# A mixture-of-experts layer whose sorted rows carry the data of both results, routed in parts of 5 and 3 sequences, with the next scan's first inputs and the last sums behind the last block

## What is computed

```python
scores = sigmoid(xf @ gate_w + bias)
top_scores, top_idx = top_k(scores, 2)
top_scores = top_scores / (sum(top_scores) + 1e-06)
w = zeros((T, 8)).at[arange(T)[:, None], top_idx].add(top_scores)
hact = gelu(einsum('th,ehi->tei', xf, up_w) + up_b)          # 8 experts, 128 -> 512
eo = einsum('tei,eih->teh', hact, down_w) + down_b           # 512 -> 128
combined = einsum('teh,te->th', eo * 0.1, w)
shared = (gelu(xf @ sw_up + sb_up) @ sw_down + sb_down) * 0.1
out = shared + combined
out = out / (max(abs(out), axis=-1) + 1e-06)                 # then x = x + 0.5 * out
```

## Time and profile before

| | us |
|---|---|
| median of 3 runs | 1491.89 (1487.93 to 1494.34) |
| the profiled execution's own time | 1493.21 |
| its span (first to last instruction) | 1490.9 |
| PE busy | 1261.4 (85%) |
| DVE busy | 967.9 (65%) |
| ACT busy | 830.7 (56%) |
| POOL busy | 685.2 (46%) |

### The profile page before, as it was taken

The page is one execution under the profiler, slowest core; times in us unless marked ns, Lnnn a source line. Parts: engine busy times, 40 slices in busy tenths (PEclk is TensorE's granted clock), DMA queues, the critical chain, the costliest instruction groups (busy, mean ns, idle before and its releaser), DMA issues. The chain is left out here.

```text
span 1490.9 us, 28176 instructions
## 1 busy us (share of the span) xinstructions
PE 1261.4 (85%) x7410; PEld 709.2 (48%) x7410; DVE 967.9 (65%) x2074; ACT 830.7 (56%) x1990; POOL 685.2 (46%) x886
## 2 busy tenths in 40 slices
PE   2896899999999969979799874598999878989992
PEld 1663222222222226747699864121222225789992
DVE  5676698988989816743133544699999985123465
ACT  0220488888888843434366672366666544356661
POOL 3121223133222121235767534388878862767652
PEclk9996699999999979969899997599899987989996
DMA  5980112222122011011487743344444422177884
GB/s 115 177 166 5 54 39 72 85 75 73 35 75 76 23 20 15 1 37 51 129 228 211 233 125 88 106 150 149 139 142 149 145 78 64 49 220 207 236 243 132
DMA packets 161927, 164.63 MB, mean 110 GB/s; under 512 B 31389, under 2 KB 113771, under 8 KB 161800
## 3 DMA queue, kind: packets, MB, share of 16 engines
q1 hardware_dynamic: 150592, 145.92, 36.0%
q0 software_dynamic: 9088, 16.94, 3.2%
q10 hardware_dynamic: 2120, 0.28, 0.2%
HBM read 115.45 MB, written 45.90 MB: 108 GB/s over the span
## 5 line engine op out<-in xcount | busy, mean ns | idle before, releaser
L1186 DVE TENSOR_REDUCE at_nm<-at_mx 128x2 f32<-128x1024 f32 x256 | 304.0, 1220 | 40.8 <-PE at_mx L1029 39.4
L1132 ACT ACTIVATE at_probs<-at_ring 128x512 f32<-128x512 f32 x512 | 269.5, 605 | 47.4 <-PE at_ring L1041 45.7
L1538 ACT ACTIVATE m_hidden<-m_pU,mw_up_b 128x128 f32<-128x128 f32 x624 | 178.0, 368 | 93.0 <-PE m_pU L1740 91.1
L1485 POOL DMA_INDIRECT pair_rows<-m_y,m_y_id x156 | 152.8, 980 | 98.8 <-DVE m_y L1684 60.8
L2230 POOL TENSOR_TENSOR ss_hc<-ss_h,ss_c_all 128x512 f32<-128x512 f32 x128 | 161.7, 1271 | 54.2 <-DVE ss_h L2400 46.9
L1749 PE MATMUL m_pD<-m_down_all,m_hidden 128*128 x1248 | 167.6, 278 | 18.3 <-ACT m_hidden L1538 17.6
L1041 PE MATMUL at_ring<-at_qq,at_kk 51*128 51x512 bf16 x512 | 163.4, 386 | 7.0 <-ACT at_probs L1132 6.1
L1740 PE MATMUL m_pU<-m_hidden,m_up_now 128*128 128x128 f32 x1248 | 168.7, 279 | 0.0
L1029 PE MATMUL at_mx<-at_kk,at_qq 48*128 48x512 bf16 x512 | 156.3, 399 | 13.2 <-DVE at_nm L1186 8.6
L2400 DVE TENSOR_TENSOR_SCAN ss_h<-ss_pA,ss_beta 128x512 f32<-128x512 f32 x128 | 155.3, 1215 | 15.5 <-ACT ss_pA L2365 6.5
L1749 PEld LDWEIGHTS m_pD<-m_down_all,m_hidden 128*128 128x128 f32 x1248 | 152.8, 193 | 20.9 <-issue 20.5
(11 more groups left out here) (311 smaller groups left out, 2007.3 us busy)
## 6 DMA issues: line engine op xcount, KB each, us to landing
m_up_now<-in_L_ffn_up_w_dram SPq DMA_DIRECT2D x156, 256.0 KB
ss_dtb<-ss_dt_rows SPq DMA_DIRECT2D x128, 256.0 KB
sorted_rows<-empty_row SPq DMA_DIRECT2D x2, 5070.0 KB, 45.6
m_xb<-sorted_rows SPq DMA_DIRECT2D x156, 65.0 KB
...
```

The costliest lines, as they stand in the source:

```text
L1132: act.activation(probs[:, (slot % 2) * GH + ORDER[j], :], ring[bank][:, :], ACT.Exp, scale=SCALE).then_inc(s.exp_done, 1)
L1186: dve.tensor_reduce(nm[group % 2][:, 2 * (pair % 2) + parity, 2 * half:2 * half + 2], mx[parity][:, :, :], AX.X, ALU.max, negate=True).the ...
L1485: pool.indirect_dma_start(pair_rows, bass.IndirectOffsetOnAxis(ap=y_id[j % Y_BUFS][:, :], axis=0), y[j % Y_BUFS][:, :], None, bounds_check ...
L1538: act.activation(hid[j % T_BUFS][:, k, :], pU[j % 2][:, k * P:(k + 1) * P], ACT.Gelu, bias=v.up_b[:, bass.ds(e, 1), k:k + 1].rearrange("p ...
```

## The change

- A row carries the data of both results: ROW is 133. Behind the 128 numbers stand the second result's id and weight (`PAIR`), the differences to the first one's (`OTHER`), and the number of the first expert (`GATE`). So `mark`, its two waits for landed DMAs and the passes go; a tile's two scatters follow each other. In each block DVE now compares the row's first expert with the block's (`is_first`) and picks id and weight (`pair`), as two linked steps ahead of the copy of the id.
- Routing is done per part. The parts hold 5 and 3 sequences (20 and 12 tiles, 47 and 31 blocks; 78 in all as before). DVE routes and places part 0, then part 1; PE makes ranks and totals after the first and after the third sequence's up product.
- POOL issues the 40 scatters of part 0, then 6 of part 1, and the other 18 one ahead of each of the first 18 written blocks.
- Five sequences are finished between blocks (a piece behind each of the blocks 53 to 77) and three behind the last. For those three PE adds the shared part and the two results into `m_pD` by matmuls with the identity (`sum_up`), and DVE reads the sum there.
- The whole lead of the scan moves behind the last block on PE, ACT, DVE, POOL and SP; only the two `take_shift` stay between blocks.

The diff, cut to its core:

```diff
-RANK_AT = 1
+RANK_AT = (0, 2)
...
-HALVES = 2
-HS, HT = NB // HALVES, NT // HALVES
...
+SPLIT = (5, 3)
...
+HT = tuple(NC * n for n in SPLIT)
+HB = tuple((2 * n * P + E1 * (P - 1)) // P for n in HT)
...
+ROW = D + 5
+PAIR, OTHER, GATE = slice(D, D + 2), slice(D + 2, D + 4), slice(D + 4, D + 5)
...
-HB = (2 * HT * P + E1 * (P - 1)) // P
-TB = HALVES * HB
 X_BUFS, Y_BUFS, T_BUFS, U_BUFS = 8, 12, 3, 6
-FINISH_AT, PIECES = 8, 5
-Y_LOAD_AT = {11: (0, 1), 18: (2,), 23: (3,)}
-LEAD_AT = {14: 3, 19: 4, 22: 5, 25: 6, 28: 7, 36: 8, 38: 9}
-SILU_AT = 23
-SHIFT_AT = {12: 0, 17: 1}
-LEAD_POOL_AT = {30: (0, 1), 31: (2,), 32: (3,), 33: (4, 5), 37: (6, 7), 38: (8,)}
+ROUTE_STEPS, RANK_STEP, LIST_STEPS = 34, 12, 4
+AHEAD = 6
+FINISH_AT, PIECES = 6, 5
+Y_LOAD_AT = {9: (0, 1), 16: (2,), 21: (3,), 26: (4,)}
+SHIFT_AT = {11: 0, 16: 1}
...
+        is_first = [sb(f"is_first{i}", [P, 1]) for i in range(2)]
+        pair = [sb(f"pair{i}", [P, 2]) for i in range(2)]
...
+                if b >= SPLIT[0] + 2:
+                    sp.wait_ge(s.summed, b - 1 - SPLIT[0])
+                elif b > 1:
+                    sp.wait_ge(s.y_added, 2 * (b - 1))
...
-            for half in range(HALVES):
-                for k in range(2):
-                    sp.wait_ge(scattered[half][k], 16 * HT)
-                for j in range(HB):
-                    load_block(half * HB + j)
-                    load_up(half * HB + j)
+            for half in range(2):
+                sp.wait_ge(scattered[half], 16 * 2 * HT[half])
...
-            if lead is not None:
-                scan_lead_stores(sp, lead)
...
             wait_written(TB)
-            for b in range(HS, NB):
+            for b in range(SPLIT[0], NB):
                 load_results(b)
+            if lead is not None:
+                scan_lead_stores(sp, lead)
...
-            def mark(half, k):
-
-                tiles = slice(half * HT, (half + 1) * HT)
-                pool.tensor_copy(v.rows[:, tiles, ID:ROW], v.idw[:, k, tiles, :]).then_inc(s.marked, 1)
-                pool.wait_ge(s.marked, 2 * half + k + 1)
...
+            def scatter(n):
+
+                tile, k = n // 2, n % 2
+                pool.indirect_dma_start(sorted_rows, bass.IndirectOffsetOnAxis(ap=index[:, k, tile:tile + 1], axis=0),
+                                        v.rows[:, tile, :], None, bounds_check=TB * P - 1, oob_is_err=False
+                                        ).then_inc(scattered[n // (2 * HT[0])], 16)
...
-            pool.wait_ge(s.weighted, 1)
-            mark(0, 0)
             pool.wait_ge(s.placed, 1)
-            for t in range(HT):
-                scatter(0, 0, t)
-            pool.wait_ge(scattered[0][0], 16 * HT)
-            mark(0, 1)
-            for t in range(HT):
-                scatter(0, 1, t)
-            mark(1, 0)
-            for t in range(HT):
-                scatter(1, 0, t)
-            pool.wait_ge(scattered[1][0], 16 * HT)
-            mark(1, 1)
-            for j in range(HB):
-                if j < HT:
-                    scatter(1, 1, j)
+            for n in range(2 * HT[0]):
+                scatter(n)
+            pool.wait_ge(s.placed, 2)
+            behind = 2 * HT[0] + AHEAD
+            for n in range(2 * HT[0], behind):
+                scatter(n)
+            for j in range(TB):
+                if behind + j < 2 * NT:
+                    scatter(behind + j)
                 put(j)
-            for j in range(HB):
-                put(HB + j)
-                if lead is not None and j in SHIFT_AT:
-                    b = SHIFT_AT[j]
+                if lead is not None and j - HB[0] in SHIFT_AT:
+                    b = SHIFT_AT[j - HB[0]]
                     take_shift(pool, g, lead, slice(b, b + 1), b)
-                if lead is not None and j in LEAD_POOL_AT:
-                    for n in LEAD_POOL_AT[j]:
-                        inputs_pool(pool, lead, 0, n)
+            if lead is not None:
+                for n in range(NS):
+                    inputs_pool(pool, lead, 0, n)
...
-                if lead is not None and j - HB in LEAD_AT:
-                    scan_lead_act(act, g, q=ahead, s=lead, t=LEAD_AT[j - HB])
+            if lead is not None:
+                for t in range(3, 10):
+                    scan_lead_act(act, g, q=ahead, s=lead, t=t)
...
+                for i, z in enumerate((logit, z2)):
+                    link(dve.tensor_reduce(top[:, T], z[:, T, :], AX.X, ALU.max))
...
+                    if i == 0:
+                        dve.tensor_copy(v.rows[:, T, D + 4], top[:, T])
+                        link(dve.scalar_tensor_tensor(out=z2[:, T, :], in0=hot[0][:, T, :], scalar=-BIG,
...
+            for half in range(2):
+                chain.begin(half)
+                choose(half)
+                put_in_place(half)
+                chain.end()
...
+            dve.tensor_scalar(gate_of[:, :], expert_f[:, :], -1.0, float(E1), ALU.mult, ALU.add)
...
+            norm = Chain(dve, s.norm_step, 4)
+            add_up = Chain(dve, s.y_added, 2)
...
+                values = pD[b % 2][:, :, :] if in_psum else acc[:, tiles, :]
+                if piece == 0 and in_psum:
+                    dve.wait_ge(s.summed, b - SPLIT[0] + 1)
+                if piece == 0 and not in_psum:
+                    add_up.begin(b)
+                    dve.wait_ge(y_in[b % 2], 32 * (b // 2 + 1))
+                    add_up.link(dve.tensor_tensor(values, values, yb[b % 2][:, 0, :, :], ALU.add))
+                if piece == 1 and not in_psum:
+                    add_up.link(dve.tensor_tensor(values, values, yb[b % 2][:, 1, :, :], ALU.add))
+                    add_up.end()
...
                     norm.begin(b)
-                    dve.wait_ge(y_in[b % 2], 32 * (b // 2 + 1))
-                    norm.link(dve.tensor_tensor(acc[:, tiles, :], acc[:, tiles, :], yb[b % 2][:, 0, :, :], ALU.add))
-                if piece == 1:
-                    dve.tensor_tensor(acc[:, tiles, :], acc[:, tiles, :], yb[b % 2][:, 1, :, :], ALU.add
-                                      ).then_inc(s.y_added, 1)
-                    dve.wait_ge(s.y_added, b + 1)
...
-                        last = dve.scalar_tensor_tensor(out=x, in0=acc[:, b * NC + c, :],
+                        last = dve.scalar_tensor_tensor(out=x, in0=values[:, c, :],
...
+            pick = Chain(dve, s.pick, 2)
             dve.wait_ge(v.loaded, BIAS_LOADS)
             e = expert_at(dve, 0)
             for j in range(TB):
...
-                dve.tensor_copy(y_id[j % Y_BUFS][:, :], xb[:, j % X_BUFS, ID:ID + 1])
+                pick.begin(j)
+                pick.link(dve.tensor_tensor(is_first[j % 2][:, :], xb[:, j % X_BUFS, GATE], gate_of[:, j:j + 1], ALU.is_equal))
+                pick.link(dve.scalar_tensor_tensor(out=pair[j % 2][:, :], in0=xb[:, j % X_BUFS, OTHER],
+                                                   scalar=is_first[j % 2][:, 0:1], in1=xb[:, j % X_BUFS, PAIR],
+                                                   op0=ALU.mult, op1=ALU.add))
+                pick.end()
+                dve.tensor_copy(y_id[j % Y_BUFS][:, :], pair[j % 2][:, 0:1])
...
-                dve.tensor_scalar(y[j % Y_BUFS][:, :], yt[j % 2][:, :], xb[:, j % X_BUFS, WEIGHT:ROW], None, ALU.mult
+                dve.tensor_scalar(y[j % Y_BUFS][:, :], yt[j % 2][:, :], pair[j % 2][:, 1:2], None, ALU.mult
                                   ).then_inc(s.y_ready, 1)
                 e = after
-                jj = j - HB - FINISH_AT
-                if 0 <= jj < HS * PIECES:
+                jj = j - HB[0] - FINISH_AT
+                if 0 <= jj < SPLIT[0] * PIECES:
                     finish(jj // PIECES, jj % PIECES)
-                if lead is not None and j - HB == SILU_AT:
-                    silu(dve, lead, 0)
-            for b in range(HS, NB):
+            for b in range(SPLIT[0], NB):
                 for piece in range(PIECES):
                     finish(b, piece)
+                if lead is not None and b == SPLIT[0]:
+                    silu(dve, lead, 0)
...
-                if t == RANK_AT:
-                    pe.wait_ge(s.step, 12)
...
+                if t in RANK_AT:
+                    half = RANK_AT.index(t)
+                    hot_rows = both[:, tiles_of(half), :].rearrange("p t e -> p e t")
+                    pe.wait_ge(s.step, ROUTE_STEPS * half + RANK_STEP)
...
-                if lead is not None and j - HB in LEAD_AT:
-                    scan_lead_pe(pe, g, q=ahead, s=lead, t=LEAD_AT[j - HB])
...
+
+            def sum_up(b):
+
+                pe.wait_ge(y_in[b % 2], 32 * (b // 2 + 1))
+                if b < SPLIT[0] + 2:
+                    pe.wait_ge(s.y_taken, TB)
+                else:
+                    pe.wait_ge(s.x_done, b - 1)
+                sums = pD[b % 2][:, :, :].rearrange("p c d -> p (c d)")
+                pe.matmul(sums, g.identf[:, :], acc[:, b * NC:(b + 1) * NC, :].rearrange("p c d -> p (c d)"),
+                          start=True, stop=False)
```

(12 more changed lines are left out.)

215 lines of the change are left out of this document (106 added, 109 removed).

## The result

The changed kernel takes **1506.84 us** (median of 6 runs, 1504.82 to 1510.98), against 1492.89 for the kernel before in the same series (6 runs). Ratio 1.0092, 95% interval 1.0063 to 1.0122: slower by about 0.9%. The forecast was 1505.2 (1487 to 1515). The profiled execution has a span of 1506.7 us, 15.8 more than before.

What follows compares the result with a forecast made beforehand. PE was taken to set the blocks' pace, with DVE nearly level where it finishes sequences. First MoE +0.8 and second +11.2 make +12.0 us on the profiled 1493.2: 1505.2 us, range 1487 to 1515.

Steps and rivals of the forecast that it cites:

- the scan stage: The scan behind the first MoE, from PE's first product on: forecast to change by 0.
- The pick: Two linked DVE steps more per block, `is_first` and `pair`: 0.42 us each block with pieces, hidden in plain blocks.
- c: Price of `is_first` and `pair` together on DVE's path per block: taken 0.42 us; 0.16 by unlinked steps, 0 if hidden.
- costs little: Rival: the two pick steps fill DVE's idle time in blocks 53 to 77; 1485.0 to 1492.7 us, chance 0.20.
- Blocks 47 to 77: Last blocks of each MoE, bound by DVE where pieces follow: −7.2 us in the first MoE, +12.0 in the second.
- The stall: Blocks 20 to 30, DVE waiting for free y because POOL writes late: goes away, −3.2 and −3.7 us.
- The start: Each MoE's start to block 0: routing −4.5, eight more scatters +10.5, mark gone −2.2, interference +1; +4.8 us, twice.
- the interference: Part 1's routing on DVE beside POOL's first scatters: +1 us per MoE, bounds 0 and 3.
- The tail of the first MoE: Behind the last block: the lead as one chain across five engines, scan's first product at 38.9 us instead of 32.5, +6.4.
- The kernel's end: Behind the second MoE's last block: sums on PE, last X 20.5 us behind the last m_y instead of 22.4, −1.9.
- The clock: Rival: PE waits in DVE-bound blocks and falls from 2.4 to 1.2 GHz; +69 us, 1574, chance 0.02.

## Why the prediction was right, and where it was not

- **The sign and the size** were right: 1506.8 for 1505.2. Part of that closeness is luck. In the profiled executions the span grew by 15.8 us where the terms add up to 12.0; the median is 1.7 below the profiled execution. And the net hides errors of both signs: the first tail (4.9), the blocks with pieces (2.3 and 1.1) and the kernel's end (0.5) were forecast too low, the starts (1.2 and 2.0) and the scan stage (1.7) too high.
- **The pick**, the forecast's deciding term: c = 0.42 by linked rows against 0.16 by unlinked ones. The trace after shows 0.42, the pick alone in the kernel before gives 9.2 us in the second MoE for 9.3 (6.4 in the first), and with the links taken off the path 0.17 is left. The rival "costs little" falls. The Trainium skill, "VectorE: DVE Perf Modes", section "The DRAIN you can't avoid", has a semaphore between chained operations as free, from eight copies that took 13.88 us either way. For two steps of one and two elements these runs show the opposite, 0.42 linked and 0.17 not. The c of 0.32 by the formula of the same page's section "The TRN2 errata — SBUF-src ops pay a fixed extra latency per instruction" falls too.
- **Blocks 47 to 77**: +14.3 for +12.0 in the second MoE, −6.1 for −7.2 in the first. One group of five blocks took 13.36 instead of 12.0; it lies where SP issues its first stores of the output, and I did not test whether they are the cause.
- **The stall** went as forecast, −3.1 and −3.7.
- **The start** was forecast 1.2 and 2.0 too dear. In the second MoE some 1 of it is the interference that I had added (+1) and that did not show, 1 the scatters' average (1.30 for 1.32, over 40), and 0.5 the routing (5.0 for 4.5); block 0 comes 0.3 later behind the last scatter, the other way.
- **The tail of the first MoE** is the step that failed: "SP issues 12 DMAs of the stack … → 37.3, and the barrier 1.6 → 38.9". The chain itself was right within 0.7 at each step up to SP's last issue, with PE's first sum at 5.1 for 4.7. What I took for the end was not: POOL's drain of 9.6 us, hidden in the kernel before and in no row of mine, ends it, and the scan begins at 43.9. I had read the 1.6 off a tail where POOL had been done for 26 us. The term was mis-sized by 4.9. Where SP does come last, with the lead's steps on DVE, the scan begins 2.3 behind its last issue, not 1.6; so 3.6 of the 4.9 are the drain, 0.7 this, and 0.7 the chain.
- **The kernel's end**, −1.4 for −1.9: there POOL is done with the last write, and its drain ends at 1493.4, ahead of the last X.
- **The clock** stayed at 1.00 with PE at 41 of 47, so DVE-bound blocks did not cost it.
